# A graph layer and a mixture of experts on one core: register loads two groups ahead, a shorter chain of far-edge steps, and a last tile added and sent in three column pieces

## What is computed

```python
edge_index = jnp.stack([src, dst])            # 20000 edges, sorted by dst
x = x + gnn(layernorm(x), edge_index, edge_type_2, ...)
x = x + ffn(layernorm(x)[None], ...)[0]

# gnn: out = norm(x) @ W_root + bias; for each of 2 relations r:
    msg = h_src @ W_rel[r] * w[:, None]
    sums = segment_sum(msg, dst, N); cnt = segment_sum(w, dst, N)
    out = out + sums / maximum(cnt, 1)[:, None]
# then elu(out) @ wo, plus the input

# ffn: 2 shared experts (mean of both) and the best 2 of 8 routed experts,
#      each gelu(x @ W1 + b1) @ W2 + b2 with 256 hidden columns
```

## Time and profile before

| | |
|---|---|
| median of 3 runs | 337.83 us (337.35 to 337.98) |
| the profiled execution | 337.76 us |
| its span, first to last instruction | 336.0 us |
| TensorE busy | 321.1 us (96%) |
| VectorE busy | 226.6 us (67%) |
| ScalarE busy | 164.8 us (49%) |
| GpSimd busy | 76.6 us (23%) |
| chain that ended last, shares | PE 69%, ACT 16%, DVE 5%, DMA 4%, issue 3% |
| TensorE's granted clock | 1.00 of full speed over the whole span |

### The profile page before, as it was taken

The page is one execution under the profiler, slowest core; times in us unless marked ns, Lnnn a source line. Parts: engine busy times, 40 slices in busy tenths (PEclk is TensorE's granted clock), DMA queues, the critical chain, the costliest instruction groups (busy, mean ns, idle before and its releaser), DMA issues.

```text
span 336.0 us, 5853 instructions
## 1 busy us (share of the span) xinstructions
PE 321.1 (96%) x1925; PEld 274.7 (82%) x1925; DVE 226.6 (67%) x436; ACT 164.8 (49%) x269; POOL 76.6 (23%) x94
## 2 busy tenths in 40 slices
PE   6999999998999999989998999999999999999994
PEld 2889897787798897869997888887888888878873
DVE  3999999976746638754557658556665565591884
ACT  2996999991131323533057575544655455610000
POOL 6750270001011010200121432222134310004840
PEclk9999999999999999999999999999999999999999
DMA  7960022000010156395051494797979982215894
GB/s 253 348 176 2 2 97 76 1 2 17 0 62 3 62 188 216 102 345 208 3 188 64 150 343 153 275 359 288 298 276 351 359 340 81 111 62 178 313 347 155
DMA packets 26752, 57.58 MB, mean 171 GB/s; under 512 B 2701, under 2 KB 16281, under 8 KB 26724
## 3 DMA queue, kind: packets, MB, share of 16 engines
q1 hardware_dynamic: 20198, 33.89, 29.6%
q0 software_dynamic: 3888, 14.16, 12.5%
q10 hardware_dynamic: 2638, 9.17, 6.9%
HBM read 66.25 MB, written 14.03 MB: 239 GB/s over the span
## 4 chain that ended last, share of the span: by engine, by line
PE 69%; ACT 16%; DVE 5%; DMA 4%; issue 3%; SPq 1%; DVEq 0%; POOL 0%; ACTq 0%
PE ps L1402 35%; PE ps L1680 17%; PE ps L1526 6%; ACT sw_raw L797 5%; PE ps L1670 4%; DMA y_acc<-in_x 4%; ACT arena_r L732 2%; ACT sw_raw L805 2%; PE ps L1561 1%; PE ps L1412 1%; PE ps L1688 1%; PE ps L1489 1%; ACT arena_r L847 1%; ACT xt L713 1%; ACT raw L769 1%
## 5 line engine op out<-in xcount | busy, mean ns | idle before, releaser
L1402 PE MATMUL ps<-arena_r 128*128 128x512 f32 (+1 forms) x264 | 67.3, 401 | 0.2 <-DVE arena_r L1132 0.2
L1680 PE MATMUL ps<-big,tile 128*128 x272 | 61.8, 380 | 1.5 <-ACT tile L908 1.0
L1402 PE MATMUL ps<-xt,arena_r 128*128 128x314 f32 (+2 forms) x312 | 59.7, 343 | 0.2 <-DVE xt L1123 0.2
L1402 PE MATMUL ps<-arena_r,xt 128*128 128x286 f32 (+1 forms) x360 | 59.0, 305 | 0.4 <-DVE arena_r L517 0.4
L1680 PEld LDWEIGHTS ps<-big,tile 128*128 128x128 f32 x272 | 51.4, 190 | 9.6 <-issue 2.2
L1402 PEld LDWEIGHTS ps<-arena_r 128*128 128x128 f32 (+1 forms) x264 | 48.0, 188 | 11.0 <-DVE arena_r L1132 0.6
L1402 PEld LDWEIGHTS ps<-xt,arena_r 128*128 128x128 f32 (+1 forms) x312 | 50.2, 187 | 6.4 <-DVE xt L1123 0.4
L637 POOL DMA_INDIRECT big<-xrow,tok_i x17 | 31.5, 1855 | 100.1 <-PE ps L1670 75.8
L1402 PEld LDWEIGHTS ps<-arena_r,xt 128*128 128x128 f32 (+1 forms) x360 | 49.2, 187 | 1.4 <-DVE arena_r L517 0.6
L938 ACT ACTIVATE arena_r<-raw 128x2048 fp32r x17 | 32.5, 1910 | 26.8 <-DMA raw<-in_L_ffn_W 16.9
L1331 DVE TENSOR_TENSOR arena_r<-raw,arena_r 128x2048 fp32r<-128x2048 f32 x17 | 38.8, 2282 | 2.1 <-ACT arena_r L938 2.1
(11 more groups left out here) (224 smaller groups left out, 383.3 us busy)
## 6 DMA issues: line engine op xcount, KB each, us to landing
big<-in_L_ffn_W SPq DMA_DIRECT2D x19, 1024.0 KB, 7.5
raw<-in_L_ffn_W SPq DMA_DIRECT2D x19, 1024.0 KB, 10.9
yrow<-work ACTq DMA_DIRECT2D x17, 512.0 KB
raw<-in_L_gnn_W_rel SPq DMA_DIRECT2D x2, 1144.0 KB, 10.6
y_acc<-in_x SPq DMA_DIRECT2D x4, 512.0 KB, 7.9
xrow<-work SPq DMA_DIRECT2D x4, 512.0 KB, 2.9
raw<-in_L_ffn_sW SPq DMA_DIRECT2D x2, 1024.0 KB, 5.9
sw_raw<-in_L_ffn_sW SPq DMA_DIRECT2D x2, 1024.0 KB
```

Source lines behind the costliest of these rows:

```text
L1402: ins = pe.matmul(out_ap, a, b, start=start and k == 0, stop=stop and k == n - 1)
L1680: ins = pe.matmul(ps[1][:, i % 2, 0:HID], xg_t[:, k * P:(k + 1) * P], big[:, bass.ds(ring * UNIT + k * HID, HID)], start=k == 0, stop=k == ...
```

## The change

Four edits.

1. VectorE's two register loads for the far loop (`far_loops(dve)`) move from behind the loop over g to the start of its turn G + 1, that is in front of the last two adds of counts. TensorE's loads stay where they are.
2. In the far loop `far_m`'s first step no longer reads `far_d`: it makes the same subtraction itself and compares the result, in one instruction. `far_u` moves behind the second step of `far_m`. The comparison of the sources is issued before the wait for `far_v`, and only the comparison of the keys behind it.
3. In the last tile both routed adds come first, and the shared part is added in three pieces of 512, 256 and 256 columns. TensorE makes the last block as two blocks of 256 columns in two banks (26 matmuls in place of 13); the second takes a bank that block 6 had.
4. SyncE stores the last tile in the same three pieces, each as soon as it is added: six DMAs in place of two.

```diff
+        LAST_COLS = (slice(0, DH), slice(DH, DH + DH // 2), slice(DH + DH // 2, D))
@@
-            for t in range(T):
-                sp.wait_ge(f_acc, 4 * t + 4)
+            pieces = [(t, 4 * t + 4, slice(0, D)) for t in range(T - 1)] \
+                + [(T - 1, 4 * T - 1 + n, cols) for n, cols in enumerate(LAST_COLS)]
+            for t, done, cols in pieces:
+                sp.wait_ge(f_acc, done)
                 for at, n in row_parts(rows[t]):
-                    sp.dma_start(out[t * P + at:t * P + at + n, :], y_acc[at:at + n, t, :]).then_inc(s_out, 16)
-            sp.wait_ge(s_out, 16 * sum(len(row_parts(r)) for r in rows))
+                    sp.dma_start(out[t * P + at:t * P + at + n, cols], y_acc[at:at + n, t, cols]).then_inc(s_out, 16)
+            sp.wait_ge(s_out, 16 * sum(len(row_parts(rows[t])) for t, _, _ in pieces))
@@
             for g in range(G + LAG):
+                if g == G + 1:
+                    windows, members = far_loops(dve)
@@
-            windows, members = far_loops(dve)
             dve.wait_ge(s_add, G)
@@
                     dve.tensor_scalar(far_d[:, :], far, w_base[:, :], None, ALU.subtract).then_inc(s_far, 1)
-                    dve.wait_ge(s_far, done + 1)
-                    dve.tensor_scalar(far_m[:, :], far_d[:, :], 0.0, None, ALU.is_ge).then_inc(s_far, 1)
-                    dve.scalar_tensor_tensor(far_u[:, :], far_d[:, :], 1.0, hr, ALU.add, ALU.add).then_inc(s_far, 1)
-                    dve.wait_ge(s_far, done + 3)
+                    dve.tensor_scalar(far_m[:, :], far, w_base[:, :], 0.0, ALU.subtract, ALU.is_ge).then_inc(s_far, 1)
+                    dve.wait_ge(s_far, done + 2)
                     dve.scalar_tensor_tensor(far_m[:, :], far_d[:, :], float(WD), far_m[:, :],
                                              ALU.is_lt, ALU.mult).then_inc(s_far, 1)
+                    dve.scalar_tensor_tensor(far_u[:, :], far_d[:, :], 1.0, hr, ALU.add, ALU.add).then_inc(s_far, 1)
                     dve.wait_ge(s_far, done + 4)
                     dve.tensor_tensor(far_v[:, :], far_u[:, :], far_m[:, :], ALU.mult).then_inc(s_far, 1)
+                    compare(src_hot[G % N_SH], iota_s, lo_t[:, bass.ds(g, 1), :].rearrange("p a c -> p (a c)"))
                     dve.wait_ge(s_far, done + 5)
-                    hots(G, lo_t[:, bass.ds(g, 1), :].rearrange("p a c -> p (a c)"), far_v[:, :]).then_inc(s_fh, 1)
+                    compare(key_hot[G % N_MH], iota_m, far_v[:, :]).then_inc(s_fh, 1)
@@
-                dve.wait_ge(f_acc, 2 * k)
+                dve.wait_ge(f_acc, 2 * k if k < 2 * T - 1 else 2 * k - 1)
@@
-            for b in range(2 * T):
+            for b in range(2 * T - 2):
                 add_routed(b)
                 add_block(b)
+            add_routed(2 * T - 2)
+            add_routed(2 * T - 1)
+            for n, cols in enumerate(LAST_COLS):
+                dve.wait_ge(f_y, 2 * T - 1 + n)
+                dve.wait_ge(f_acc, 4 * T - 2 + n)
+                bank = ps[2 + n // 2][0:rows[-1], n % 2, 0:cols.stop - cols.start]
+                dve.tensor_tensor(y_acc[0:rows[-1], T - 1, cols], y_acc[0:rows[-1], T - 1, cols], bank,
+                                  ALU.add).then_inc(f_acc, 1)
@@
+            def shared_down(o, t, cols):
+
+                tokens = slice(t * P, t * P + rows[t])
+                hilo(o, [((ht_hl[0][:, KH * e + m, tokens], ht_hl[1][:, KH * e + m, tokens]),
+                          (sw2_hl[e][0][:, m, cols], sw2_hl[e][1][:, m, cols]))
+                         for e in range(NS) for m in range(KH)], stop=False)
+                pe.matmul(o, w_t[:, tokens], b2_hl[:, cols], start=False, stop=True).then_inc(f_y, 1)
@@
             for b in range(2 * T):
+                if b < 2 * T - 1:
+                    shared_down(o, t, slice(h * DH, (h + 1) * DH))
+                else:
+                    shared_down(o[:, 0:DH // 2], t, LAST_COLS[1])
+                    pe.wait_ge(f_acc, 2 * (b - 3) + 2)
+                    shared_down(ps[3][0:rows[t], 0, 0:DH // 2], t, LAST_COLS[2])
```

More of the change, by code:

```diff
@@ L1041, in _, with compare @@
             split_rows_lo(2, 2)
-            def hots(n, lo, key, both=True):
[L1045 to L1049, removed]
+            def compare(hot, columns, index):
+                shape = [CE, CG // 2, columns.shape[1], 2]
+                return dve.tensor_tensor(
+                    hot, columns[0:CE].rearrange("p (q k) c -> p q k c", q=1).to_broadcast(shape),
+                    index.rearrange("p (q a c) -> p q a c", a=1, c=2).to_broadcast(shape), ALU.is_equal)
+            def hots(n, lo, key, both=True):
                 if both:
@@ L1739, in _ @@
             pe.wait_ge(r_x, NT)
+            def shared_down(o, t, cols):
[3 more added lines that the diff above has]
+                         for e in range(NS) for m in range(KH)], stop=False)
+                if t == 0 and cols.start == 0:
+                    pe.wait_ge(s_wts, 1)
+                    pe.wait_ge(s_b2lo, 1)
+                pe.matmul(o, w_t[:, tokens], b2_hl[:, cols], start=False, stop=True).then_inc(f_y, 1)
             for b in range(2 * T):
                 t, h = block_of(b)
-                cols = slice(t * P, t * P + rows[t])
                 o = ps[2 + b % 4 // 2][0:rows[t], b % 2, :]
```

## The result

The changed kernel took 336.38 us (median of 6 runs, 335.72 to 336.69); the kernel before, beside it, 337.89 us (6 runs, 337.35 to 338.29). The ratio is 0.9955, interval 0.9942 to 0.9968: 1.5 us less, 1.1 to 2.0 by the interval.

What follows compares the result with a forecast made beforehand. VectorE's queue was taken to bound the far block, with TensorE right behind, and the final adds and sends the end. Far block 0.45 plus last tile 0.80 gave 1.25 us off 337.83: 336.6 us, own range 336.1 to 337.1.

Steps and rivals of the forecast that it cites:

- Register loads: Far-edge block, VectorE: loads moved ahead of the last two adds gain 0.28 of 1.28 us; bounds 0 and 0.88.
- Three steps: Far loop, VectorE: three dependent steps in place of four gain 0.20 us; bounds 0 and 0.40.
- TensorE's cap: Far counts: TensorE idles 0.42 us behind `root(1)`, limiting the second comparison's 0.48 us; 0.45 taken.
- Everything behind shifts whole: After the far block: TensorE or DMAs issued relative to it release the rest, so the 0.45 us arrives whole.
- rival A: Far block brings nothing: later steps give it back or a DMA replaces the wait; 337.0 us, 14% chance.
- The last tile: End of kernel: routed adds in a row, three pieces, six DMAs; gain 0.8 us, bounds +0.38 (loss) and -1.05.
- Rival C: Last tile, TensorE: weight loads don't shorten with the columns, pairs keep 0.231 us; slower, 338.9 us, 5% chance.
- Rival B: Tail costs by its last issue, not its bytes, the whole 3.51 us; 337.8 us, 11% chance.
- The far block's 0.45: Far-edge block: gain taken for moved loads and shorter chain together, 0.45 us.
- The tail's 0.80: Last tile's adds and sends in pieces: gain taken, 0.80 us.
- the cover lost at the tenth gather: Last tile, VectorE: tenth routed add no longer has an add of 0.69 us ahead, so it waits until 329.25.

Runs made afterwards that it cites:

- the far block alone: Kernel before with only edits 1 and 2 (register loads ahead, shorter far chain), last tile as before: 336.75 us, ratio 0.9986 (0.9978 to 0.9995).

## Why the prediction came out right

**Register loads.** Expected for add 39 behind add 37 was 2.01 us, measured 2.02; for the loop's first operation 2.58, measured 2.59. That a moved load isn't free, because the adds are queued behind it in the same sequencer, was the step that decided the size: 0.28 of 1.28 us, measured 0.27 to 0.29.

**Three steps.** Here the term was a little too small: 0.20, measured 0.26. From the loop's first operation to the second comparison it was 1.79 us and is 1.52, where my steps gave 1.59. The source comparison follows `far_v` by 0.11 us (73.80 to 73.91) and not by 0.15; the 0.34 to the second comparison held.

**TensorE's cap.** I read 0.42 us of idle time between two records and allowed "a little more". It was 0.56: the counts start 0.13 to 0.15 us before the record of the group ahead ends. So the 0.45 that I took was 0.09 low in the trace (0.54), and within the interval of the far block's own runs (0.47, 0.17 to 0.74).

**Everything behind shifts whole.** The medians bear this out (0.47 off for the far block alone), but a single pair of traces doesn't show it. TensorE runs 1.15 us earlier than before at 76 to 216 us, and 0.36 from 231.6 on. (The 1.15 are 0.6 that were there at 24 us and 0.54 of the far block.) What changes there is a wait of TensorE for the load of a 1 MB weight tile. The issue of it by SyncE, and TensorE behind it, in before:

```profile
220.31 0.38 SPq L481 DMA_DIRECT2D big<-in_L_ffn_W  x1
...
231.62 0.69 PE L1680 MATMUL ps<-big,tile 128*128 x2 [0.48 <-issue]
```

and in the changed kernel (issue; then the wait in the list of waits: us, times, longest):

```profile
219.19 0.38 SPq L482 DMA_DIRECT2D big<-in_L_ffn_W  x1
...
PE ps L1693 <- issue: 1.2, 1, 1.2
```

The load was issued 1.12 us earlier but landed only 0.36 earlier (11.9 us behind its issue, against 11.1). With the far block alone the same wait is 0.35 us, and its lead passes whole:

```profile
231.02 1.34 PE L1682 MATMUL ps<-big,tile 128*128 x5 [0.35 <-issue]
```

So that landing varies from run to run, and it isn't a wall that gives the gain back: rival A, a DMA further on that takes the place of the wait, had a place, but its price was not 0.45. VectorE has such a place of its own: in this pair its lead falls from 0.31 us at the first routed add to 0.01 at the second, which waits 0.41 us for its gather. The medians, not this pair, say what came through.

**The last tile.** VectorE: I expected a wait of 0.28 us for the tenth gather; it was none, or 0.7. The last 112-row issue was expected 5.30 us behind the start of the ninth routed add (332.88 less 327.58) and came 4.96 and 5.58 behind it. Piece adds of 0.69 and 0.42 us with 0.1 between them came as predicted. TensorE's line in the changed kernel (ns min/median/max, first and last start):

```profile
L1415 PE MATMUL ps<-xt,arena_r x24: 276/280/285, 328.3 to 331.1; 128*113 128x256 f32 x24
L1415 PEld LDWEIGHTS ps<-xt,arena_r x23: 174/175/180, 328.3 to 331.0; 128*113 128x113 f32 x23
```

Twenty-four matmuls start within 2.8 us, 0.118 apart, though each load of weights is booked with 175 ns. Rival C is refuted: two of them, which replace one of 512 columns, took 0.24 us and not 0.46, and TensorE's last matmul ends at 331.49, 0.1 us before the last add starts. (By its own steps C's time was 338.8 and not 338.9.) The sentence of the Trainium skill ("TensorE: Matmul & The Clock Gate", section "The mechanism") that would have made it true does not describe these rows; the same section also lets a load into the background weight buffer go ahead of running matmuls, and with that the rows agree.

SyncE: expected 0.38 us from one issue to the next, measured 0.35 to 0.39. Expected from the last 112-row issue to the end 2.32 us (335.2 less 332.88), measured 2.31 and 2.32. The 0.25 us that I put on top for small packets and the one-row DMA was not worked out from any row; the measured surcharge over the old pace is 0.23, so this hit is in part luck, and with the one-row DMA gone from SyncE's queue the way to the end is 2.46 us, not shorter. Rival B, a fixed 3.5 us per send, is refuted by the series 3.50, 2.90, 2.31. The estimate by the Trainium skill ("DMA: Bandwidth & Descriptors", section "Anatomy of one DMA — SWDGE (gpsimd) path") had 0.78 us for the fewer bytes (0.80 with the 463 KB that 113 rows are, where the prediction has 452); measured are 1.20 (3.51 less 2.31). The page's two figures were measured for GpSimd's DMAs; for these of SyncE the measurement decides, and what makes up the other 0.4 us no run here shows.

So the sum of 1.25 us lies between the two measurements of the changed kernel, 1.5 and 1.05. The far block's 0.45 holds by its mechanism (0.47 in time, 0.54 in the trace). The tail's 0.80 doesn't hold as a fixed term: by itself it measured 0.40, and the traces give 0.1 to 0.5 with a late gather and 0.7 to 1.15 with an early one. The mis-sized term is the cover lost at the tenth gather, 0.28 on paper and 0 or 0.7 on the chip. That 0.28 lies between the two is luck: it was the landing time of one profile, and that time moves by more than the term.

## What to carry to other kernels

Moving a register load ahead gains only what is not queued behind it in the same sequencer: count from the place where it lands, and see whether the engine that waits for the result has idle time left. The end of a kernel gets shorter with its last piece (here 0.6 us for each halving), so cut the last piece small, but count every issue of the queue that sends it (here 0.35 to 0.39 us each, also for one row), and try to give left-over rows to a queue that is idle. A landing time read from one profile is one draw: before a cover is removed, ask what it hides on a bad draw, and compare it with the same stretch in several traces.

## What the runs showed of the hardware

- A matmul may start 0.13 to 0.16 us before the record of the group ahead of it on TensorE ends (far counts behind `root(1)`, in all traces of kernels with both far-block edits); the idle time between two records understates what can be won by that much.
- The GpSimd issue of an indirect gather takes 0.93 to 0.94 us, but where it starts 0.11 to 1.15 us behind the start of a routed add of VectorE (1.28 us, 1024 columns) it ends 0.01 to 0.02 us behind the end of the block add that follows, up to 1.98 us after its start (68 of 130 issues in thirteen traces, without exception); one that starts at most 0.09 us behind the add takes 0.94. The tenth gather lands up to 4 us apart (325.9 to 330.3).
- The load of one 1 MB weight tile, issued at about 220 us, landed 10.5 to 11.9 us later in all traces, where the others of its kind took about 5.5.
- From the issue of a SyncE store of 112 rows to the end of the span pass 3.5 us for 1024 columns, 2.9 for 512 and 2.3 for 256. The last landing is 0.42 us ahead of that end.
